# Scan layers: B and C in four column tiles over quarters of the tokens, diagonals loaded by pairs, residual moved by halves

## What is computed

```
z = W_proj xn + b_proj                      # rows: 192 x, 192 delta, 16 B, 16 C
delta = softplus(z_delta + dt_bias)
h_t = exp(delta_t * A) * h_(t-1) + (delta_t * x_t) * B_t      # per channel, 16 states
y_t = sum over states of h_t * C_t, + x_t * D
out = x + W_out y + b_out
```

## Time and profile before

| | |
|---|---|
| median of three runs | 4197.12 us |
| the profiled execution | 4211.27 us, span 4209.5 us |
| TensorE matmul busy | 3749.5 us, 89% of the span |
| VectorE busy | 3086.7 us, 73% |
| GpSimd busy | 2309.8 us, 55% |
| ScalarE busy | 2041.0 us, 48% |
| transfers | 453.11 MB, 108 GB/s in the mean |
| granted TensorE clock, mean | 0.958 |

### The profile page before, as it was taken

How to read it: one execution, slowest core, us unless ns; L and a number is a source line. 1 busy time by engine, 2 the same in 40 slices (tenths; PEclk the granted TensorE clock), 3 DMA queues, 4 the chain that set the end, 5 groups by cost and what they waited for, 6 DMA issues and landing times.

```text
span 4209.5 us, 120863 instructions
## 1 busy us (share of the span) xinstructions
PE 3749.5 (89%) x49136; PEld 2316.1 (55%) x49136; DVE 3086.7 (73%) x3557; ACT 2041.0 (48%) x2707; POOL 2309.8 (55%) x877
## 2 busy tenths in 40 slices
PE   4995799899899898499999999999999999999998
PEld 4994666666666666245444444554555454444444
DVE  6564667667657665378887888888888788888887
ACT  2332344444444443265555555555665555555553
POOL 1111121121121120188888888888888888888887
PEclk9997899999999999699999999999999999999999
DMA  9724133233233232436555555556565555555643
GB/s 100 90 45 111 55 102 107 71 101 108 71 96 113 71 93 55 115 89 137 131 113 121 126 119 124 117 124 145 113 143 113 131 131 119 122 119 124 146 104 92
DMA packets 346994, 453.11 MB, mean 108 GB/s; under 512 B 64649, under 2 KB 218893, under 8 KB 346433
## 3 DMA queue, kind: packets, MB, share of 16 engines
q1 hardware_dynamic: 345104, 444.06, 47.0%
q10 hardware_dynamic: 1362, 1.39, 0.1%
HBM read 301.69 MB, written 94.37 MB: 94 GB/s over the span
## 4 chain that ended last, share of the span: by engine, by line
PE 30%; SPq 11%; issue 6%; DMA 5%; POOL 4%; DVE 3%; ACT 1%; DVEq 0%; POOLq 0%; ACTq 0%
PE ssm_u_ps L861 11%; PE ssm_y_ps L874 10%; SPq L766 6%; PE ssm_scratch L891 4%; DMA ssm_b_diag<-ssm_b_blocks 4%; POOL ssm_h L1256 3%; DVE ssm_h L1173 2%; PE ssm_u_ps L936 2%; SPq L747 2%; PE ssm_scratch L901 1%; SPq L736 1%; SPq L717 1%; PE ssm_scratch L916 1%; DMA ssm_b_blocks<-ssm_b_t 1%; SPq L723 1%
## 5 line engine op out<-in xcount | busy, mean ns | idle before, releaser
L1256 POOL TENSOR_TENSOR ssm_h<-ssm_h,ssm_c_rep 128x2048 f32<-128x2048 f32 x384 | 1752.9, 4570 | 231.6 <-DVE ssm_h L1173 203.2
L1173 DVE TENSOR_TENSOR_SCAN ssm_h<-ssm_decay,ssm_h,ssm_u_ps 128x512 f32<-128x512 f32 x768 | 935.8, 1260 | 211.6 <-PE ssm_u_ps L861 211.6
L861 PEld LDWEIGHTS ssm_u_ps<-ssm_b_diag,ssm_dx_t 64*64 64x64 f32 x24576 | 754.2, 136 | 550.1 <-issue 538.0
L861 PE MATMUL ssm_u_ps<-ssm_b_diag,ssm_dx_t 64*64 64x128 f32 x24576 | 936.6, 292 | 128.1 <-DMA ssm_b_diag<-ssm_b_blocks 78.9
L1173 DVE TENSOR_TENSOR_SCAN ssm_h<-ssm_decay,ssm_u_ps 128x512 f32<-128x512 f32 x768 | 892.1, 1203 | 131.0 <-PE ssm_u_ps L861 103.8
L1010 ACT ACTIVATE ssm_decay<-ssm_delta_rep,ssm_a_neg 128x1024 f32<-128x1024 f32 x768 | 849.6, 1144 | 226.7 <-DVE ssm_h L1173 212.0
L874 PE MATMUL ssm_y_ps<-ssm_h,ssm_state_sum 128*64 128x512 f32 x3072 | 773.6, 626 | 6.1 <-POOL ssm_h L1256 6.1
L1783 ACT ACTIVATE l_probs<-l_work 128x532 f32<-128x532 f32 (+1 forms) x384 | 217.3, 566 | 558.5 <-PE l_work L1637 551.8
L874 PEld LDWEIGHTS ssm_y_ps<-ssm_h,ssm_state_sum 128*64 128x64 f32 x3072 | 191.8, 140 | 319.7 <-issue 309.0
L1952 DVE RECIPROCAL l_den<-l_den 96x1024 f32<-96x1024 f32 x32 | 209.6, 6548 | 194.2 <-ACT l_den L1796 194.2
L2035 POOL TENSOR_TENSOR l_rstd<-l_var_eps,l_minus_half 96x2 f32<-96x2 f32 x16 | 11.1, 693 | 585.7 <-DVE l_var_eps L1872 585.7
(11 more groups left out here) (162 smaller groups left out, 5340.9 us busy)
## 6 DMA issues: line engine op xcount, KB each, us to landing
ssm_c_rep<-ssm_c_by_state SPq DMA_DIRECT2D x256, 512.0 KB, 7.0
ssm_delta_rep<-ssm_delta SPq DMA_DIRECT2D x384, 128.0 KB, 3.6
l_qk_parts<-l_qk SPq DMA_DIRECT2D x48, 768.0 KB, 4.7
ssm_b_diag<-ssm_b_blocks SPq DMA_DIRECT2D x1024, 32.0 KB, 3.2
ssm_x<-x_after_l SPq DMA_DIRECT2D x32, 768.0 KB, 6.1
ssm_x_res<-x_after_l SPq DMA_DIRECT2D x192, 128.0 KB, 4.4
l_x<-x SPq DMA_DIRECT2D x64, 192.0 KB, 9.0
x_after_l<-l_x SPq DMA_DIRECT2D x64, 192.0 KB, 4.1
```

Source lines behind the costliest of these rows:

```text
L861: made = nc.tensor.matmul(u_ps[64 * par:64 * par + 64, ring("u", w), r, at:at + 128], dx_t[rows, db, 2 * win + k, 64 * g:64 * g + 64], of_ ...
L1173: nc.vector.tensor_tensor_scan(h[:, s % S_RING, npi, t], decay[:, 2 * (s % 2) + npi, t], u, start, ALU.mult, ALU.add).then_inc(scanned, 1)
L1256: nc.gpsimd.tensor_tensor(view, view, c_rep[:, 2 * q:2 * q + 2, :], ALU.mult).then_inc(c_applied, 1)
```

## The change

B and C are projected with one weight tile of 32 columns (16 rows of B, 16 of C) for four quarters of 256 tokens, one quarter in each of four column tiles, where before each of four column tiles took B or C for 512 tokens. The results are copied by two activations of 128 by 256 instead of three, B and C together are turned in two transposes of 128 by 128 instead of four of 64 by 128, and C is stored in four transfers instead of two. The diagonals of two groups npq come in one set of eight transfers of 64 KB each: pair 0 before C 0, pair 1 after C 1. So 16 transfers take the place of 32. A pair waits until the last fill that reads either of its groups is over, and the fill for group 2 now waits for the transfers of groups 2 and 3. The residual is loaded and stored in two transfers of 384 KB each instead of six of 128 KB.

```diff
--- before.py
+++ after.py
...
@@ -517,9 +518,9 @@
         dx = sb("dx", [128, HALF])
         dx_t = sb("dx_t", [128, 3, 4, 128])
         x_kept = sb("x_kept", [128, HALF])
-        b_rows = sb("b_rows", [64, HALF])
+        bc_rows = sb("bc_rows", [128, 256])
         b_t = sb("b_t", [128, 4, 32])
-        c_rows = sb("c_rows", [128, HALF])
+        c_rows = sb("c_rows", [128, 256])
         b_diag = sb("b_diag", [128, 4, 64, 32])
         delta_rep = sb("delta_rep", [128, 3, L])
         c_rep = sb("c_rep", [128, 8, L])
@@ -528,7 +529,7 @@
         y_sb = sb("y_sb", [128, 2, 3, HALF])
         w_delta = [sb(f"w_delta_{i}", [C + 1, 2, 192]) for i in range(2)]
         w_x = [sb(f"w_x_{i}", [C + 1, 2, 192]) for i in range(2)]
-        w_bc = [sb(f"w_bc_{i}", [C + 1, 2, 64]) for i in range(2)]
+        w_bc = [sb(f"w_bc_{i}", [C + 1, 2, 32]) for i in range(2)]
         w_out = [sb(f"w_out_{i}", [128, 3, 3, 128]) for i in range(2)]
         d_skip = [sb(f"d_skip_{i}", [128, 3]) for i in range(2)]
         a_neg = sb("a_neg", [128, 2, 24])
@@ -690,7 +691,7 @@
 
         def of_part(npq, rows, win, k, g, par):
 
-            first = 16 * win + 8 * k + 4 * g + 2 * par
+            first = 16 * k + 8 * win + 4 * g + 2 * par
             return b_diag[rows, npq, :, first:first + 2]
 
         def res_rows(t, e):
@@ -713,20 +714,19 @@
 
                 def load_residual(n):
                     for e in range(2):
-                        for q in range(3):
-                            sp.dma_start(x_res[64 * e:64 * e + 64, q, :], res_rows(image(sources, n), e)[:, q]).then_inc(res_loaded, 16)
+                        sp.dma_start(x_res[64 * e:64 * e + 64, :, :], res_rows(image(sources, n), e)).then_inc(res_loaded, 16)
 
                 def store(n):
                     sp.wait_ge(res_added, n.count(3, 3))
                     for e in range(2):
-                        for q in range(3):
-                            sp.dma_start(res_rows(image(targets, n), e)[:, q], x_res[64 * e:64 * e + 64, q, :]).then_inc(out_stored, 16)
+                        sp.dma_start(res_rows(image(targets, n), e), x_res[64 * e:64 * e + 64, :, :]).then_inc(out_stored, 16)
 
                 def store_c(n):
                     await_drained(sp, fill(n, "bc"))
-                    for g in range(2):
-                        sp.dma_start(of_half(c_dram[n.s], g),
-                                     by_run(c_rows[64 + 32 * g:80 + 32 * g, :])).then_inc(c_stored, 16)
+                    for i in range(4):
+                        win, g = divmod(i, 2)
+                        sp.dma_start(of_half(c_dram[n.s], g)[:, 2 * win:2 * win + 2],
+                                     c_rows[32 * i + 16:32 * i + 32, :].rearrange("p (a z) -> p a z", a=2)).then_inc(c_stored, 16)
 
                 def load_c(n, q):
                     if not n.first:
@@ -749,23 +749,25 @@
 
                 def store_b(n):
                     if not n.first:
-                        for npq in range(4):
-                            sp.wait_ge(diag_loaded[npq], n.count(128, 0))
+                        for pair in range(2):
+                            sp.wait_ge(diag_loaded[pair], n.count(128, 0))
                             sp.sem_inc(b_store_seen, 1)
                     sp.wait_ge(b_kept, n.count(1, 1))
                     sp.dma_start(b_dram[:, :, 0:32].rearrange("q p v -> p q v"), b_t[:, :, :]).then_inc(b_stored, 16)
 
-                def load_diagonal(n, npq):
+                def load_diagonals(n, pair):
+
                     if not n.first:
-                        sp.wait_ge(u_filled, before(n).count(8 * S_STEPS, 8 * (8 + npq) + 8))
+                        sp.wait_ge(u_filled, before(n).count(8 * S_STEPS, 8 * (9 + 2 * pair) + 8))
                         sp.sem_inc(diag_read, 1)
-                    flat_rows = b_dram[npq].rearrange("p v -> (p v)")
+                    two = slice(2 * pair, 2 * pair + 2)
+                    flat_rows = b_dram[two].rearrange("q p v -> q (p v)")
                     for blk in range(128 // BLOCK):
                         first = blk * BLOCK * (BLOCK * 32 + 32)
                         j0 = BLOCK * blk % 64
-                        sp.dma_start(b_diag[BLOCK * blk:BLOCK * (blk + 1), npq, j0:j0 + BLOCK, :].rearrange("p j v -> p (j v)"),
-                                     flat_rows[first:first + BLOCK * BLOCK * 32].rearrange("(p v) -> p v", p=BLOCK)
-                                     ).then_inc(diag_loaded[npq], 16)
+                        sp.dma_start(b_diag[BLOCK * blk:BLOCK * (blk + 1), two, j0:j0 + BLOCK, :].rearrange("p q j v -> p q (j v)"),
+                                     flat_rows[:, first:first + BLOCK * BLOCK * 32].rearrange("q (p v) -> p q v", p=BLOCK)
+                                     ).then_inc(diag_loaded[pair], 16)
 
                 def prologue(n):
                     load(n)
@@ -789,13 +791,11 @@
                     store_b(n)
                     sp.wait_ge(diag_cleared, 1)
                     sp.wait_ge(b_stored, 16)
-                    load_diagonal(n, 0)
-                    sp.wait_ge(c_stored, 32)
+                    load_diagonals(n, 0)
+                    sp.wait_ge(c_stored, C_LANDED)
                     load_c(n, 0)
-                    load_diagonal(n, 1)
+                    load_diagonals(n, 1)
                     load_c(n, 1)
-                    load_diagonal(n, 2)
-                    load_diagonal(n, 3)
 
                 def early(n):
                     load_c(n, 2)
@@ -813,29 +813,27 @@
                         sp.wait_ge(xn_made, m.count(1, 1))
                         load(after(m))
                     if not n.first:
-                        sp.wait_ge(out_stored, n.count(96, 0))
+                        sp.wait_ge(out_stored, n.count(32, 0))
                         load_residual(n)
                     if not is_last(n):
                         store_c(m)
                         load_delta(m, 0)
                         store_b(m)
-                        sp.wait_ge(c_stored, m.count(32, 32))
+                        sp.wait_ge(c_stored, m.count(C_LANDED, C_LANDED))
                         sp.sem_inc(c_store_seen, 1)
                         sp.wait_ge(b_stored, m.count(16, 16))
                         sp.sem_inc(b_store_seen, 1)
-                        load_diagonal(m, 0)
+                        load_diagonals(m, 0)
                         load_c(m, 0)
-                        load_diagonal(m, 1)
                         sp.wait_ge(decay_made, n.count(TILES_S, 16))
                         sp.sem_inc(rep_free, 1)
                         load_delta(m, 1)
-                        load_diagonal(m, 2)
                         load_c(m, 1)
-                        load_diagonal(m, 3)
+                        load_diagonals(m, 1)
 
                 def tail(n):
                     store(n)
-                    sp.wait_ge(out_stored, n.count(96, 96))
+                    sp.wait_ge(out_stored, n.count(32, 32))
 
                 schedule(sp, prologue, early, late, tail)
 
@@ -848,7 +846,7 @@
                     if npq == 0 and win == 0:
                         await_drained(pe, fill(n, f"dx.{db}"))
                     if db == 0 and win == 0:
-                        pe.wait_ge(diag_loaded[npq], n.count(128, 128))
+                        pe.wait_ge(diag_loaded[npq // 2], n.count(128, 128))
                     if not (n.first and w < U_RING):
                         await_place(pe, n, "u", w)
                         pe.sem_inc(window_free, 1)
@@ -897,17 +895,17 @@
                     pe.wait_ge(xn_made, n.count(1, 1))
                     for ci in range(2):
                         for i in range(4):
-                            which, g = divmod(i, 2)
-                            last = nc.tensor.matmul(scratch[32 * i:32 * i + 32, :], w_bc[n.layer][:, ci, 32 * which:32 * which + 32],
-                                                    xn[:, ci, g, :], start=(ci == 0), stop=(ci == 1))
+                            win, g = divmod(i, 2)
+                            last = nc.tensor.matmul(scratch[32 * i:32 * i + 32, 0:256], w_bc[n.layer][:, ci, :],
+                                                    xn[:, ci, g, 256 * win:256 * win + 256], start=(ci == 0), stop=(ci == 1))
                     last.then_inc(filled, 1)
 
                 def turn_b(n):
 
                     pe.wait_ge(bc_kept, n.count(1, 1))
                     pe.sem_inc(rows_seen, 1)
-                    for k in range(4):
-                        last = nc.tensor.transpose(scratch[:, 64 * k:64 * k + 64], b_rows[:, 128 * k:128 * k + 128], ident[0:64, 0:64])
+                    for k in range(2):
+                        last = nc.tensor.transpose(scratch[:, 128 * k:128 * k + 128], bc_rows[:, 128 * k:128 * k + 128], ident[:, :])
                     last.then_inc(filled, 1)
 
                 def turn_dx(n, db):
@@ -1054,18 +1052,16 @@
                 def take_bc(n):
```

(24 more changed lines are left out.)

## The result

The changed kernel takes 4153.62 us, the median of 4 runs (4148.75 to 4159.45), the kernel before 4202.34 us, now also of 4 (4193.46 to 4213.19): 49 us less. The ratio on record is 0.9873, 95% interval 0.9849 to 0.9898, clear of noise; the two medians by themselves give 0.9884, which lies inside. The profiled execution has a span of 4146.9 us against 4209.5.

A forecast was written before the change was run, and what follows sets the result against it. TensorE was taken to set each pass, held up by one late diagonal transfer. Terms of -31 (TensorE), -6 (waits) and +4 us (clock) sum to -33: 4211.3 us profiled becomes 4178, forecast as 4164 us; range 4085 to 4210.

The forecast's parts named there:

- Rivals B: The wait of TensorE's fills for diagonals goes away altogether: 4070 us, chance 0.20.
- rival C: Merged second pair lands later relative to its need, behind the second C load; wait grows: 4235 us, chance 0.15.
- D: Projection is bound by issue and gains nothing, the wait keeps its size: 4197 us, chance 0.15.
- Projection and turn: TensorE's B and C projection gains 0.90 us, transposes of B 0.1: 1.0 us a pass, 31 us over 31 passes.
- the 0.4 us of loss: Some 60 cycles per matmul, if unhidden, would take 0.4 us of the projection's 0.95 us gain, the sum 12 us poorer.
- SyncE: 22 issues of 68 fewer a pass; last diagonal issue 9.5 us earlier, first pair starting at t = 15.0.
- Landing: Second pair of diagonals lands at t = 36.1 to 38.4, middle 37.3; fill 4 waits 0.1 to 2.4 us, middle 1.3.
- The gain in waiting: TensorE's wait for diagonals moves from fill 6 to fill 4, 0.2 us less a pass, 6 us over 29 passes.
- Clock: Half clock after waits a little more frequent: 4 us against the change, bounds 15 us lost and 20 us gained.
- Start and end: Prologue and final stores of the 32 passes move 2 us either way: counted as nothing.
- The 6.5 us of earlier need: Fill 4 needs the second pair at t = 36.0, where fill 6 needed the last diagonals at 42.5.
- the 9.5 us of earlier issue: SyncE finishes issuing the diagonals at t = 28.4, where before the last issue was at 37.9.

The follow-up runs named there:

- the TensorE part alone: Kernel before with only the projection in quarters, two transposes and four C stores; diagonals singly, residual by thirds: 4218.84 us, ratio 1.0016.
- the halves alone: Kernel before with only the residual loaded and stored in two transfers each: 4127.06 us, ratio 0.9817.
- the pairs alone: Kernel before with only the diagonals loaded by pairs, with their waits and order: 4231.79 us, ratio 1.0043.
- the pair first: Changed kernel with the second pair of diagonals loaded ahead of the second C load: 4067.39 us, ratio 0.9664.
- the old TensorE part: The pair first, but with the projection over 512 columns, four transposes and two C stores put back: 4095.79 us, ratio 0.9713.
- y kept later: The pair first, but VectorE adds the first block's y behind the scan of window 12 instead of 11: 4037.67 us, ratio 0.9584.
- the residual by thirds: The pair first, but with the residual by thirds again instead of halves: 4125.11 us, ratio 0.9794.
- the half of C ahead: Changed kernel with one of the second C load's two transfers ahead of the second pair, the other behind it: 4122.61 us, ratio 0.9776.

## Why the prediction was right

The direction, the place of the new wait and the time hold: 4164 us was forecast, 4153.62 came, within the range and the forecast's own. Rivals B, C and D did not come. The way the time was put together does not hold, and that the sum is so close is partly luck. The steps:

- **Projection and turn.** The fill behind the projection starts 1.00 us after it for 1.86 before, a gain of 0.86 us for the 0.90 that I took; the 0.4 us of loss that the prediction names beside this term did not show. The turn gained next to nothing: to the next fill 0.37 us for 0.39. I had halved the row of four transposes of 128 columns, 0.33 us; the two take 0.44. Together TensorE saves 27 us of work for 31.
- **SyncE.** The first pair comes at t = 14.9 for 15.0 forecast. The last pair is issued from 24.6 to 29.5 for 24.3 to 28.4, as it took 4.9 us to issue for 4.1.
- **Landing.** Fill 4 starts at t = 38.1 in the quiet pass, in the range of 36.1 to 38.4 and 0.8 us behind its middle. The wait is 1.86 us for 1.3 forecast, against 1.46 before at fill 6.
- **The gain in waiting is the term that was mis-sized.** I carried 0.2 us from the quiet pass to all, 6 us; the rows say 103.9 - 80.6 = 23 us. In the timelines of 30 passes the wait of the last fill kept its size: 68.1 us at fill 6 before, 62.4 at fill 4 after. What went besides are 14.5 us at fill 2, in 15 of the 30 passes, which the prediction saw go, "but only into this one".
- **A quiet pass was the wrong sample.** In the quiet pass fill 6 started at t = 43.9 before and fill 4 at 38.1 after, 5.8 us earlier with 5.4 asked back: 0.4 us. In the mean of the 29 passes that wait, these are 45.5 and 38.4, 7.1 us earlier: 1.7 us a pass, some 50 us. The quiet pass became 0.2 us shorter (71.37 to 71.14), the mean of 30 passes 1.8 us (75.7 to 73.9), where the prediction had about 1.
- **Clock.** TensorE's busy time, 71.21 us a pass before and 70.13 after in the mean of 30, fell by 0.2 us beyond the projection. I put that down to the granted clock: some 6 us given back, where I had put 4 against the change.
- **Start and end** are 11 us shorter (first pass 71.9 us for 78.7, the stretch from the last projection to the end 111.0 for 115.0), where I had put nothing.
- **The profiled sum**: 55 us less in 30 passes, 11 less at both ends, 3 us more in the layers ahead of them: 63 us for the 33 forecast. The medians differ by 49.

What misleads most is the split. The terms read as if TensorE brought 31 us and SyncE 6, "all on the path". By the prediction's own account the wait is set by a landing, and TensorE's saving doesn't move it. The runs of the parts bear this out: the TensorE part alone gave 1.0016, the halves alone 0.9817. The change without its TensorE part was not run. The 6.5 us of earlier need and the 9.5 us of earlier issue were the pairs and the halves in one difference: by themselves one is a loss and the other a gain larger than the change. And where rival C takes issue time as small against the transfer, neither view holds alone: from the kernel before, 8 issues fewer in larger transfers gain 1.8%, and in the changed kernel bytes decide.

## What to carry to other kernels

Where every pass of a loop waits for the same transfer, price each part of a change by how far it moves the end of that wait, not by the work it takes off the busiest engine: work saved ahead of the wait comes back as waiting. Before transfers are merged, look at which reader gets its data later and which bytes then stand in front. Here a small urgent transfer was moved ahead of a large one that is needed only five us later (in the pass shown fill 4 starts at t = 36.2, and GpSimd uses the second group of C at 41.4); that gave 2.1%, more than any merging. Take the wait's size from all passes, not from a quiet one.

## What the runs showed of the hardware

- TensorE stands idle inside fills, at a few fixed places of the program, in the changed kernels mostly near t = 47, for a reason that the profile doesn't show. The row "issue" at the fills' line reads 7.3 us before, 5.6 in the TensorE part alone, 1.4 in the pairs alone, 13.7 in the halves alone, 6.5 in the change, 12.9 with the pair first, 11.3 and 12.8 in its variants with the old TensorE part and with y kept later, and 31.9 and 30.6 in the residual by thirds and in the half of C ahead. In those last two the queues move 218 GB/s or more during most of these waits. Instructions that arrive late behind the data would fit, but no run shows it, and full queues alone don't bring the wait. In the TensorE part alone the queues move over 190 GB/s in all of 30 passes while TensorE is at the places that wait most in those two runs, and its waits there come to 1.5 us in all.
- A wait of 6.09 us in the pairs-alone kernel and the granted clock: it is 0.50, 1.2 of 2.4 GHz, in the rows from 3860 to 3866 us. It fell before the wait ended at 3861.61 us, and the fill behind it took 1.98 us for 1.21.

```profile
3861.61 1.98 PE L859 MATMUL ssm_u_ps<-ssm_b_diag,ssm_dx_t 64*64 64x128 f32 x32 [6.09 <-DMA ssm_b_diag<-ssm_b_blocks]
```

```profile
3860.00:3862.00 2.00, 0.39 (x8) 0.42 (x12) 0.00 (x0) 0.00 (x0) 0.00 (x0) 0.50 1.03 227
3862.00:3864.00 2.00, 2.00 (x34) 1.48 (x28) 0.00 (x0) 0.00 (x0) 0.00 (x0) 0.50 1.02 225
3864.00:3866.00 2.00, 2.00 (x6) 0.47 (x4) 0.00 (x0) 0.00 (x0) 0.00 (x0) 0.50 1.04 229
```

- What an issue on SyncE takes depends little on the bytes. Eight diagonal transfers take 3.56 us at 32 KB each and 3.59 at 64 KB, so 0.45 us each; two residual loads of 384 KB take 1.29 us, two C loads of 512 KB 1.25, and six residual loads of 128 KB 3.69 us, so 0.6 each.
